# A scan kernel on one Trainium2 core: the A product's sum as a fourth accumulating transfer, and ScalarE's normalising moved ahead of its copies of the next chunk's inputs

## The reference

```python
def _L0_ffn_ref(x, W, V, gamma, beta):
    Wx = batchnorm(jnp.einsum('bti,hi->bth', x, W))      # 3136 tokens
    def step(yt, wx_t):
        yt = jax.nn.sigmoid(wx_t + yt @ V.T)
        return (yt, yt)
    ...

def _L1_conv_ref(x_ri, Wf, bf, Wi, bi, Wd, bd, A_real, ...):
    forget_gate = jax.nn.sigmoid(x_ri @ Wf + bf + 2.0)
    input_gate = jax.nn.sigmoid(x_ri @ Wi + bi)
    delta = jax.nn.softplus(x_ri @ Wd + bd) * 0.1
    ...                                  # Ar, Ai, Br, Bi: bounded spectra of two 7x7 kernels
    Bx_r = Br * x_r - Bi_ * x_i
    Bx_i = Br * x_i + Bi_ * x_r
    inp = delta * input_gate * Bx
    def step(h_state, _):                # 16 times, from zero
        Ah_r = Ar * h_r - Ai * h_i
        Ah_i = Ar * h_i + Ai * h_r
        return ((fg_r * Ah_r + inp_r, fg_i * Ah_i + inp_i), None)
```

## Time and profile before

| | |
|---|---|
| median of 3 runs | 13171.84 us (13164.88 to 13181.59) |
| profiled execution | 13158.25 us, span 13156.4 us |
| scan stage in it | 5291.7 us (first tanh) to about 11490 us |
| busy over the span | PE 71%, DVE 77%, ACT 70%, POOL 41% |

### The profile page before, as it was taken

One profiled execution on the slowest core, in us unless ns is written; L12 is line 12 of the kernel. 1 busy time (PEld: TensorE's weight loads), 2 busy tenths in 40 slices (PEclk: granted clock), 3 DMA queues, 4 the chain that ended last, 5 costly groups with the idle time before them and its releaser, 6 DMA issues. The chain is left out here.

```text
span 13156.4 us, 223254 instructions
## 1 busy us (share of the span) xinstructions
PE 9385.1 (71%) x77110; PEld 6941.7 (53%) x77110; DVE 10185.1 (77%) x22621; ACT 9159.4 (70%) x21851; POOL 5332.7 (41%) x4855
## 2 busy tenths in 40 slices
PE   7888888888888887766666666666666665255544
PEld 5666666666766665544444444444444443133343
DVE  6777777777777775388888888888888889899910
ACT  6888888888888886466667666666666666477711
POOL 4444444454444444122222322222222223188866
PEclk9999999999999998676766666666767666677755
DMA  3333333333333332244444444444444444476544
GB/s 72 80 80 80 85 86 85 84 80 80 80 80 80 85 85 67 59 105 106 103 109 103 109 100 107 105 100 109 102 108 104 109 97 95 63 141 125 98 80 70
DMA packets 1451133, 1215.62 MB, mean 92 GB/s; under 512 B 65493, under 2 KB 1337368, under 8 KB 1399844
## 3 DMA queue, kind: packets, MB, share of 16 engines
q1 hardware_dynamic: 1290212, 653.81, 21.5%
q0 software_dynamic: 103232, 444.75, 18.7%
q10 hardware_dynamic: 56576, 102.79, 2.3%
HBM read 567.56 MB, written 325.32 MB: 68 GB/s over the span
## 5 line engine op out<-in xcount | busy, mean ns | idle before, releaser
L1282 PEld LDWEIGHTS s_pW<-s_XU,s_vh 128*128 128x128 f32 x6272 | 1451.6, 263 | 2039.1 <-ACT s_XU L1156 1758.7
L1282 PE MATMUL s_pW<-s_XU,s_vh 128*128 128x64 f32 x6272 | 1523.5, 336 | 1132.1 <-ACT s_XU L1156 1117.2
L1156 ACT ACTIVATE s_XU<-s_pW 128x64 f32<-128x64 f32 x3136 | 715.0, 228 | 1179.0 <-PE s_pW L1282 1146.8
L1311 PE MATMUL s_pG<-s_wg,s_XNT 128*128 128x384 f32 (+1 forms) x3200 | 1491.0, 554 | 8.2 <-ACT s_Z L1128 8.2
L414 ACT ACTIVATE KB<-pV,qkb 32x392 f32<-32x392 f32 x2048 | 1188.1, 580 | 25.0 <-PE pV L504 1.1
L254 POOL TENSOR_TENSOR SS<-SS,mx 128x784 f32<-128x784 f32 x512 | 768.8, 1502 | 800.2 <-DVE mx L347 800.1
L1172 ACT ACTIVATE s_f<-s_X,s_nmr,s_rst 128x128 f32<-128x128 f32 (+1 forms) x1600 | 654.1, 485 | 559.8 <-POOL s_nmr L862 559.8
L262 POOL TENSOR_TENSOR XR<-XR,pbias 112x512 f32<-112x512 f32 x448 | 570.5, 1274 | 665.3 <-DMA XR<-in_x_dram 665.3
L466 ACT ACTIVATE XH<-XR,nm,rs 112x128 f32<-112x128 f32 x1792 | 731.2, 482 | 104.3 <-POOL nm L273 96.0
L1269 PE MATMUL s_pN<-s_ident,s_f 128*128 128x128 f32 (+1 forms) x800 | 211.0, 418 | 826.1 <-issue 437.9
L512 PE MATMUL pS<-KB,QT 128*64 128x196 f32 x8192 | 793.7, 336 | 0.0
(11 more groups left out here) (261 smaller groups left out, 28894.7 us busy)
## 6 DMA issues: line engine op xcount, KB each, us to landing
XL<-in_x_dram SPq DMA_DIRECT2D x64, 1568.0 KB, 12.5
XR<-in_x_dram SPq DMA_DIRECT2D x64, 1568.0 KB, 18.3
x_dram<-XR SPq DMA_DIRECT2D x64, 1568.0 KB, 8.1
xh_dram<-XH SPq DMA_DIRECT2D x64, 1568.0 KB, 8.2
e_X<-out_dram SPq DMA_DIRECT2D x64, 1568.0 KB, 16.0
s_XQ<-xh_dram ACTq DMA_DIRECT2D x384, 256.0 KB, 4.5
s_X<-x_dram POOLq DMA_DIRECT2D x96, 1024.0 KB, 8.1
s_BX<-s_Dl POOLq DMA_DIRECT2D x96, 1024.0 KB, 7.0
```

What stands on the lines that cost most here:

```text
L1156: act.activation(XU[j % 2][:, t, :], pW[t // R % 2][:, B * (t % R):B * (t % R) + B], ACT.Tanh, scale=0.5).then_inc(u_sb, 1)
L1282: pe.matmul(pW[t // R % 2][:, B * (t % R):B * (t % R) + B], vh[:], before, start=False, stop=True, skip_group_check=True).then_inc(z_ps, 1)
L1311: pe.matmul(pG[i % 3][0:tc, 0:3 * C], XNT[:, i, 0:tc], wg[:], start=True, stop=True).then_inc(g_ps, 1)
```

## The change

The A product's turned part goes to the tile `Z` instead of `Dl`. VectorE's addition of the two parts (line 1042) is gone; GpSimd issues an accumulating transfer from `Z` into `Wv` behind the deviation and ahead of the B product's. The product with the forget gate moves behind two operations of the powers and waits for that transfer, and the first gate pair waits for that product, since it overwrites `Z` and the former gates. ScalarE normalises from step 3 on in slots 1 to 3 (step 10 stays in slot 0), its copies of the next chunk's inputs move from steps 1, 4, 7, 10 to 10, 12, 14, 16 in these slots, and the squares move: 6 to 8, 8 to 10, 14 to 12, 16 to 14, 20 to 18, 22 to 20. In slot 0 GpSimd issues `add_x1` ahead of `add_input`.

```diff
+        def first_normal(s):
+            return 10 if s == 0 else 3
+        def turning(s, k, after):
+            first, step = (0, 3) if s == 0 else (9, 2)
+            q, r = divmod(k - after - first, step)
+            return q if r == 0 and 0 <= q < NQ else None
...
+                if oc is not None and s == 0:
+                    add_x1(oc)
                 if o is not None and o >= 1:
                     add_input(o - 1)
-                if oc is not None and s == 0:
-                    add_x1(oc)
...
+                if o is not None:
+                    pool.wait_ge(wp_d, o + 1)
+                    pool.dma_start(Wv[0:tm].rearrange("t r b c -> t (r b c)"), Z[0:tm].rearrange("t r b c -> t (r b c)"),
+                                   accum_op=ALU.add).then_inc(wv_d, 16)
...
-                    turned_by(tm, Wv, inp, a, wp_d)
-                    dve.wait_ge(wp_d, o + 1)
-                    dve.tensor_tensor(flat(wv), flat(wv), flat(dl), ALU.add).then_inc(wv_d, 1)
-                    dve.wait_ge(am, o * NA + 3)
+                    turned_by(tm, Wv, Z, inp, a, wp_d)
+                    dve.wait_ge(am, o * NA + 1)
                     did(dve.scalar_tensor_tensor(t1, d0, -2.0, t1, ALU.mult, ALU.subtract))
-                    dve.wait_ge(wv_d, o + 1)
-                    did(dve.scalar_tensor_tensor(flat(wv), flat(tf), 1.0, flat(wv), ALU.add, ALU.mult))
...
                     did(dve.scalar_tensor_tensor(f1[:, 1], t1, -1.0, d1, ALU.add, ALU.mult))
                     did(dve.scalar_tensor_tensor(f0[:, 0], f0[:, 0], -0.25, d0, ALU.add, ALU.add))
+                    dve.wait_ge(wv_d, (o + 1) * 16)
+                    did(dve.scalar_tensor_tensor(flat(wv), flat(tf), 1.0, flat(wv), ALU.add, ALU.mult))
...
                 if i == 0:
-                    wait(act, dv, (oc - 1) * NV + 9)
+                    wait(act, dv, (oc - 1) * NV + 12)
...
-                    if prep and k in (1, 4, 7, 10):
-                        keep_turned(j, s, k // 3)
-                    if conv and 10 <= k < 10 + NQ:
-                        q = k - 10
+                    if prep and turning(s, k, 1) is not None:
+                        keep_turned(j, s, turning(s, k, 1))
+                    if conv and 0 <= k - first_normal(s) < NQ:
+                        q = k - first_normal(s)
```

More of the change, by code:

```diff
@@ L931, in rows, with turned_by @@
                 return v.rearrange("t r b c -> t r (b c)")
-            def turned_by(tc, out, of, coef, part_sem):
+            def turned_by(tc, out, part, of, coef, part_sem):
                 def by(first):
@@ L1174, in _ @@
                         w.then_inc(xn_d, 1)
-                    if o is not None and k == 6:
+                    if o is not None and k == 8:
                         needs(4)
@@ L1178, in _ @@
                         act.activation(f0[:, 0], t0, ACT.Square, bias=cols[0:tm, 1:2]).then_inc(am, 1)
-                    if o is not None and k == 8:
+                    if o is not None and k == 10:
                         act.activation(d1, d0, ACT.Square).then_inc(am, 1)
-                    if o is not None and k == 14:
+                    if o is not None and k == 12:
                         act.wait_ge(am, o * NA + 3)
@@ L1195, in _ @@
                                        ACT.Identity, bias=cols[:, 0:1]).then_inc(n_sb, 1)
-                    if o is not None and k == 16:
+                    if o is not None and k == 14:
                         needs(8)
                         act.activation(t2, t1, ACT.Square).then_inc(am, 1)
-                    if o is not None and k == 20:
+                    if o is not None and k == 18:
                         if conv:
@@ L1203, in _ @@
                         act.activation(f1[:, 0], t1, ACT.Square, bias=cols[0:tm, 2:3]).then_inc(am, 1)
-                    if o is not None and k == 22:
-                        needs(11)
+                    if o is not None and k == 20:
+                        needs(10)
                         act.wait_ge(am, o * NA + 6)
@@ L1259, in turn_inputs @@
                 if oc is not None:
-                    wait(pe, n_sb, oc * NQ)
+                    wait(pe, n_sb, (oc + (s > 0)) * NQ)
                 for b in range(Q):
@@ L1296, in _ @@
                         turn_u(oc + 1, (k - 17) // 2)
-                    if prep and k in (0, 3, 6, 9):
-                        turn_inputs(j, s, k // 3, oc)
-                    if conv and 11 <= k < 11 + NQ:
-                        if k == 11:
+                    if prep and turning(s, k, 0) is not None:
+                        turn_inputs(j, s, turning(s, k, 0), oc)
+                    if conv and 0 <= k - first_normal(s) - 1 < NQ:
+                        q = k - first_normal(s) - 1
+                        if q == 0:
                             if scan and s == NO - 2:
                                 pe.wait_ge(raw_d, j + 1)
-                            if prep:
-                                pe.wait_ge(xt_sb, ((j + 1) * NO + s) * NQ + NQ)
-                        turn_normal(oc, tc, k - 11)
+                            pe.wait_ge(xt_sb, min((j + 1) * NO + s + (s == 0), NCH * NO) * NQ)
+                        turn_normal(oc, tc, q)
                     if conv and k >= K - OS:
```

11 lines of the change are left out of this document (5 added, 6 removed).

## The result

The changed kernel takes 13775.74 us (median of 4 runs, 13768.25 to 13783.39) against 13168.36 us for the kernel before, measured beside it. The ratio is 1.046, with an interval from 1.0441 to 1.0478: 607 us slower.

A forecast was written before the change was run, and what follows sets the result against it. VectorE bounds one slot of four, ScalarE's list the other three. Slot changes +7.5, +8.7, +6.4, -1.5 give +21.1 a chunk, 485 us for 23 chunks, plus 10: 13653, stated as 13660; range 13300 to 13900.

The forecast's parts named there:

- N moves only to the deviation: N, ScalarE's first normalising instruction, comes 1.7, 0 and 4.1 us sooner after D, VectorE's slot start, in slots 1 to 3.
- The fifth square at N + 21.5: Slots 1 to 3: ScalarE's fifth square ends 21.5 us after its first normalising instruction; bounds 17.4 and 27.4.
- ScalarE without waits: Rival: no waits for TensorE and loads, fifth square at its lower bound, N + 17.4; about 13380 us, 12 in 100.
- The first gate pair at N + 27.2: Slots 1 to 3: G, the first gate pair, follows fifth square, three operations and gate product; before, N + 12.1.
- The seventh square at G + 5.1, or 3.95 in slot 3: ScalarE's seventh square ends 5.1 us after the first gate pair in slots 1 and 2, 3.95 in slot 3.
- The rival of late loads: Loads of the next inputs land late; at 10.4 us each the time is 14070 us; 6 in 100.
- VectorE's tail: VectorE's need from the seventh square to the next slot's start: 21.3, 22.7 and 16.4 us in slots 1, 2, 3.
- The slots: Slots 1, 2 and 3 take 62.9, 71.3 and 54.55 us, rises of 7.5, 8.7 and 6.4.
- Slot 0: Normalising keeps its step and add_x1 goes first: the slot takes 74.3 us against 75.8, -1.5.
- The sum: +21.1 us a chunk for 23 chunks, 485 us, plus 10 for the last two: 13653, stated as 13660.
- The cover of 7 us: A product's transfer lands at D + 24 or 25, its reader not before D + 31; gone if ScalarE were 7 us sooner.
- VectorE stays the bound and 290 us go: Rival: engines keep up and the addition's saving shows, 12880 us; decided at fifth square N + 14.5; 8 in 100.

The follow-up runs named there:

- A third buffer: Changed kernel with three buffers instead of two for the next chunk's inputs, each load issued one copy sooner: 13660.49 us, 1.0379 to the kernel before.
- the last experiment: Kernel before with add_x1 first, deviation ahead of B spectrum, sixth and seventh squares sooner, A product's sum by transfer, gate product directly behind B product: 12727.01 us, 0.9663.
- the list alone: Kernel before with only ScalarE's and TensorE's new order (also called the order alone); addition, product's place and GpSimd's order kept: 13600.41 us, 1.0339.
- the late product alone: Kernel before with only the A product's sum as a transfer, later gate product and gate pair's wait (also called the transfer alone): 13451.21 us, 1.0227.
- the three parts: ScalarE's and TensorE's order, the transfer with late product, and add_x1 first, each alone on the kernel before: together +527 us, whole change +607.
- the old places and the transfer: Changed kernel with normalising and input copies back at their old steps in all slots, transfer and late product kept: 13270.41 us, 1.0086 to the kernel before.
- the kernel with GpSimd's order alone: Kernel before with add_x1 issued ahead of add_input in slot 0, nothing else: 12937.34 us, 0.9837.

## Why the prediction was right

The forecast was 13660 with a range from 13300 to 13900; the time is 13775.74. Step by step, measured in the changed kernel:

- **N moves only to the deviation.** Right: N = D + 9.3, 16.4 and 7.0 in slots 1, 2 and 3, against 9.3, 16.3 and 7.0. ScalarE's idle time ahead of it was 7.1 us in slot 1 and 7.2 in slot 3, not 10, since it reached step 3 later than I had it; the end of the wait is what counts.
- **The fifth square at N + 21.5.** Right: N + 21.8, 22.0 and 21.5. The lower bound of 17.4, ScalarE without waits, was not reached in any run with this order, so that rival falls. The third quarter's load landed in time for this step.
- **The first gate pair at N + 27.2.** It came at N + 28.1, 28.3 and 27.3. The mechanism, a product behind three operations behind the fifth square, holds in slot 3. In slots 1 and 2 the last quarter's load was as late as the product.
- **The seventh square at G + 5.1, or 3.95 in slot 3.** This term was mis-sized: G + 7.45 and 6.5 in slots 1 and 2, and 4.0 in slot 3. The forecast weighs the landing of the third quarter's load and leaves out the fourth's. The third, issued at 8206.45, landed in time after 2.7 us. The fourth, issued at 8210.05 with the B product's transfer 0.93 us ahead of it, took 7.5, between the median of 4.5 and the slowest of 10.4 that the forecast allowed the third. TensorE stands still for it, the next scan steps are not ready behind G, and the square comes 1.4 to 2.4 us late. A third buffer gave G + 5.2. The rival of late loads is thus true in a part: some 80 us, at a place where the forecast had not looked. (Its three terms for slot 3 add to 3.9 and not 3.95.)
- **VectorE's tail.** Right: 21.3, 22.8 and 16.45 us.
- **The slots.** The medians are 66.3, 74.0 and 54.8 us, against 62.9, 71.3 and 54.55 forecast.
- **Slot 0.** The statistics began at D + 17.5 (8396.11 less 8378.61), forecast 17.35, and G at N + 19.3, forecast 19.2. N came at D + 25.9 and not 29.4, since I had taken the deviation's 7.9 us over from before, and it took 3.9. The slot is 71.3 us, forecast 74.3. That the total comes as near as it does is in part luck: slots 1 and 2 came out 6.1 us longer together than forecast and slot 0 3.0 shorter.
- **The sum.** A chunk rose by 24.7 us, not 21.1; for 23 chunks this is 568. Another 22 lie ahead of the stage: its first tanh was at 5291.7 in the profiled execution of before and at 5313.5 in that of the changed kernel. The change touches nothing there, and in the experiments' kernels, eight of which hold the transfer, it stood at 5283.1 to 5302.7, so I don't count this as the change's. What holds ahead of the stage in one execution is left open. That leaves 21 for the first and the last two chunks, where I had 10. (13653 and 13.6 make 13667, where the forecast says 13660; it changes nothing.)

Of the signs named, those on VectorE's busy time (down 207 us, forecast 229), the waits for the first and the fifth square (the fifth 5.9 us in slot 1, about 6 forecast), and the transfer that lands before its reader asks were seen. The cover of 7 us shows in the last experiment: with the transfer's reader directly behind the B product the wait for it comes to 48 us in 35 slots.

What the prediction did not separate is why the time is lost. It added 15 us from N to G (27.2 less 12.1) and put them down to ScalarE's list and the three operations behind the fifth square in one. The runs part them: the list alone makes N + 24.3 and costs 446 us, the late product alone makes N + 17.4 and costs 297. The two rises, 12.2 and 5.3 us, nearly add up in the changed kernel (N + 28.1, where their sum gives 29.6). The 54 to 80 us by which the three parts fall short of the whole are about the size of what the third buffer gave back, and TensorE's wait for loads is 3.2 us in the order alone, 28.0 in the transfer alone and 172.2 in the changed kernel (145.6 with the old places and the transfer, at other steps). This fits late loads as a part that needs order and transfer together; it is not shown, since a third buffer was not tried on each part.

The rival on the other side, VectorE stays the bound and 290 us go, was to decide at the fifth square by N + 14.5. In the last experiment that is so (N + 11.5, and G at N + 14.0), and still the saving does not show: 12727 with the transfer, 12691 without. VectorE's 2.2 us a slot are given back in waits, 48.0 us for the transfer and, in VectorE's list of waits with the transfer and without it, for the normalising:

```profile
DVE s_BX L944 <- ACT s_f L1173: 246.2, 94, 10.9
DVE s_BX L939 <- ACT s_f L1172: 17.7, 4, 10.9
```

With the addition gone, ScalarE's normalising ends last again.

## What to carry to other kernels

In an engine's list, a wait is a wait for everything behind it: before an item is moved forward, look up when its last input is ready, and count what would stand behind it until then. Here N could move by 4 us at the most, and the work put behind it moved the first gate pair 12 us further from N. When work is moved to a transfer, the place of its reader and of whoever waits for that reader is the cost to work out; the transfer gained nothing clear, and its reader's place cost 282 us. Of two transfers issued together, issue the one first whose landing has a chain behind it: this order was the one gain in the change, 217 us on the kernel before, nearly half of it from a shorter deviation.

## What the runs showed of the hardware

**Two accumulating transfers issued together.** The one issued second pays. In the kernel before, `add_x1` followed `add_input` by 1.3 us, and its reader started 13.0 us after its issue. In the changed kernel it is issued 0.54 us ahead, and its reader starts after 8.2 us; the reader of `add_input` now starts 13.3 us after its issue (8388.47 to 8401.78). The stage's median for `add_x1` is 8.0 us from issue to landing.

**GpSimd's short operations stretch beside VectorE.** The three operations of the deviation took 2.19, 4.86 and 0.67 us in slot 0 before, and 0.21, 2.93 and 0.55 in the changed kernel, where VectorE waited for a transfer when they began; in the kernel with GpSimd's order alone they took 0.21, 2.93 and 0.60. The second of them in the kernel before, and what VectorE ran beside the first two:

```profile
8111.76 4.86 POOL L860 TENSOR_TENSOR s_rst<-s_rst,s_nhalf 128x16 f32<-128x16 f32 x1
8109.32 2.28 DVE L939 TENSOR_TENSOR s_Wv<-s_IN,s_par_a 128x2048 f32<-128x2048 f32 x1
8111.53 2.30 DVE L940 TENSOR_TENSOR s_Dl<-s_IN,s_par_a 128x2048 f32<-128x2048 f32 x1
```

GpSimd's first operation (8109.49, 2.19 us) ends at 8111.68, 0.08 us behind the end of line 939 at 8111.60, and its second, begun 0.23 us into line 940, takes 1.93 us more than where VectorE was waiting when it began. The Trainium skill, in "SBUF — State Buffer", section "SBUF: two separate sides", says that the two engines share one pair of ports as an exclusive lock, held for a whole instruction by an operation of GpSimd or by one of VectorE with two inputs in SBUF. The trace agrees for GpSimd's waits. For the other direction it does not: in the changed kernel line 954 began at 8401.78, while GpSimd's second operation ran from 8400.59 to 8403.52, and took its usual 2.29 us. No experiment took the two apart.
